# The sums of absolute values of the third feed-forward weight, made by VectorE instead of ScalarE

## What is computed

```python
def _quantize(w):
    gamma = jnp.mean(jnp.abs(w))
    return jnp.clip(jnp.round(w / (gamma + EPS)), -1.0, 1.0)
def _bitlinear(x, w):
    return jnp.matmul(x, _quantize(w).T)
...
x1 = _bitlinear(x, w1)
x2 = _bitlinear(x, w2)
hidden = jax.nn.sigmoid(x1) * x2
return _bitlinear(hidden, w3)
...
x = _layernorm(x + _L0_attn_ref(x, Wq, bq, Wk, bk, Wv, bv, Wo, bo), axis=-1)
x = _layernorm(x + _L0_ffn_ref(x, w1, w2, w3), axis=-1)
```

## Time and profile before

| what | us |
|---|---|
| median of 3 runs | 677.97 |
| lowest and highest run | 674.71, 678.23 |
| the profiled execution | 679.64 |
| its span in the trace | 677.7 |
| TensorE busy in it | 628.8 |
| VectorE busy | 465.6 |
| ScalarE busy | 353.4 |
| GpSimd busy | 133.8 |

### The profile page before, as it was taken

How to read it: one execution, slowest core, us unless ns; L and a number is a source line. 1 busy time by engine, 2 the same in 40 slices (tenths; PEclk the granted TensorE clock), 3 DMA queues, 4 the chain that set the end, 5 groups by cost and what they waited for, 6 DMA issues and landing times.

```text
span 677.7 us, 10688 instructions
## 1 busy us (share of the span) xinstructions
PE 628.8 (93%) x3342; PEld 343.6 (51%) x3342; DVE 465.6 (69%) x795; ACT 353.4 (52%) x814; POOL 133.8 (20%) x148
## 2 busy tenths in 40 slices
PE   6767858799999999999999999999999999999996
PEld 2544545435656565534556565534656565544442
DVE  2767676568877985567878885678878885655333
ACT  2677695514857674313767584313767575303320
POOL 1209678321000400022000400122000400110001
PEclk9689998999999999999999999999999999999999
DMA  7660523020221120021221130020231110000001
GB/s 272 222 222 24 209 60 128 1 59 4 68 93 29 48 78 1 34 70 26 58 88 44 34 92 1 32 71 25 55 86 49 28 36 0 28 21 15 1 1 62
DMA packets 20509, 41.95 MB, mean 62 GB/s; under 512 B 4704, under 2 KB 5856, under 8 KB 19936
## 3 DMA queue, kind: packets, MB, share of 16 engines
q1 hardware_dynamic: 19488, 39.86, 19.3%
q10 hardware_dynamic: 960, 1.33, 0.5%
HBM read 20.20 MB, written 4.19 MB: 36 GB/s over the span
## 4 chain that ended last, share of the span: by engine, by line
PE 76%; DVE 9%; issue 6%; ACT 3%; DMA 3%; SPq 1%; POOL 1%; DVEq 0%; POOLq 0%; ACTq 0%
PE t_ps L1010 15%; PE b_ps L970 11%; PE a_ps L970 11%; PE c_ps L1063 8%; PE a_ps L924 7%; PE s_ps L999 7%; PE a_ps L985 6%; PE b_ps L985 5%; PE a_ps L948 2%; DMA late<-in_w 2%; DVE sh_sb L738 2%; SPq L310 1%; DVE stat L698 1%; ACT p_sb L508 1%; DVE late L728 1%
## 5 line engine op out<-in xcount | busy, mean ns | idle before, releaser
L508 ACT ACTIVATE p_sb<-s_ps,sh_sb 128x512 f32<-128x512 f32 x240 | 164.4, 688 | 86.3 <-DVE sh_sb L738 86.2
L738 DVE TENSOR_REDUCE sh_sb<-s_ps 128x1 f32<-128x512 f32 x240 | 157.5, 679 | 1.9 <-PE s_ps L999 1.9
L1010 PE MATMUL t_ps<-table_sb,p_sb 128*128 128x128 f32 x1024 | 140.4, 281 | 19.4 <-ACT pt_sb L516 16.7
L1010 PEld LDWEIGHTS t_ps<-table_sb,p_sb 128*128 128x128 f32 x1024 | 120.9, 144 | 59.1 <-ACT p_sb L508 24.8
L745 DVE COPY pt_sb<-t_ps 128x512 f32<-128x512 f32 x128 | 88.2, 689 | 85.8 <-PE t_ps L1010 84.3
L516 ACT ACTIVATE pt_sb<-t_ps 128x512 f32<-128x512 f32 x128 | 76.4, 597 | 57.9 <-PE t_ps L1010 56.1
L999 PE MATMUL s_ps<-k_st,q_st 128*128 128x512 f32 x240 | 90.3, 458 | 4.3 <-DVE k_st L659 2.5
L970 PE MATMUL a_ps<-late,q 128*128 128x512 f16 x344 | 81.6, 380 | 2.0 <-DVE late L674 2.0
L970 PE MATMUL b_ps<-late,q 128*128 128x512 f16 x352 | 83.5, 380 | 0.0
L385 POOL TENSOR_TENSOR rot<-raw,table_sb 128x512 f32<-128x512 f32 x20 | 25.5, 1277 | 248.4 <-ACT raw L475 233.3
L924 PE MATMUL a_ps<-xT_sb,wq_sb 128*128 128x512 f32 x128 | 63.1, 624 | 7.6 <-DMA wq_sb<-in_wq 6.3
(11 more groups left out here) (96 smaller groups left out, 623.9 us busy)
## 6 DMA issues: line engine op xcount, KB each, us to landing
q_st<-hi SPq DMA_DIRECT2D x128, 64.0 KB, 2.0
q_st<-lo SPq DMA_DIRECT2D x128, 64.0 KB, 2.0
late<-in_w SPq DMA_DIRECT2D x2, 2816.0 KB, 12.0
xT_sb<-in_xT SPq DMA_DIRECT2D x8, 512.0 KB, 4.7
late<-in_x SPq DMA_DIRECT2D x4, 1024.0 KB, 5.5
out<-late SPq DMA_DIRECT2D x16, 256.0 KB, 2.0
late<-in_w SPq DMA_DIRECT2D x2, 1408.0 KB, 7.2
wo_sb<-in_wo SPq DMA_DIRECT2D x1, 1024.0 KB, 5.7
```

Of the source, the lines that this page charges most:

```text
L508: act.activation(p_sb[:, h % 2, t, :], score_bank(b, n), ACT.Exp, bias=sh_sb[:, n % (2 * SR):n % (2 * SR) + 1], scale=-1.0, accum_out=sums ...
L738: dve.tensor_reduce(sh_sb[:, n % (2 * SR):n % (2 * SR) + 1], score_bank(b, n), AX.X, ALU.min).then_inc(maxed, 1)
L1010: mm = pe.transpose(t_ps[k % 2][:, t * P:(t + 1) * P], p_sb[:, h % 2, t, k * P:(k + 1) * P], id_sb)
```

## The change

The third weight's four sums leave ScalarE's program. VectorE gets a function `abs3_sum`, a TENSOR_REDUCE with absolute value over a piece, and runs it in pairs at the end of its heads 9 and 10. It counts on a semaphore of its own, and TensorE's `total(2)` waits for that one. No elementwise result is written any more for this weight. The sums of the first two weights stay where they were.

```diff
-ABS_AT = [0, 0, 1, 1, 2, 3, 4, 5, 9, 9, 10, 10]
+ABS_AT = [0, 0, 1, 1, 2, 3, 4, 5]
+ABS3_AT = [9, 9, 10, 10]
...
+        abs3_summed = sem("abs3_summed")
...
+            def abs3_sum(c):
+
+                if c == 0:
+                    dve.wait_ge(w_ffn[2], 16)
+                dve.tensor_reduce(asum[:, 2, c:c + 1], piece(stage[2], c, SUMS), AX.X, ALU.add,
+                                  apply_absolute_value=True).then_inc(abs3_summed, 1)
+
...
+                    if h in ABS3_AT:
+                        abs3_sum(ABS3_AT.index(h))
+                        abs3_sum(ABS3_AT.index(h) + 1)
                     if h in TOTAL_AT:
                         thresholds(TOTAL_AT.index(h))
...
-                pe.wait_ge(abs_summed, (n + 1) * SUMS)
+                if n < 2:
+                    pe.wait_ge(abs_summed, (n + 1) * SUMS)
+                else:
+                    pe.wait_ge(abs3_summed, SUMS)
```

## The result

The changed kernel takes 682.17 us (median of 5 runs, 681.75 to 683.72) against 677.62 for the kernel before (5 runs, 674.71 to 678.23). The ratio is 1.0093 with a 95% interval of 1.0074 to 1.0112: slower by a little under 1%, and clear of the scatter. By the medians the change costs 4.1 to 4.6 us, where +3.6 was forecast, and both medians lie inside the range of 677.5 to 686.0. The ratio of the first session would even make 6.3 us (5.0 to 7.6 by its interval), that of the second 4.3 (2.9 to 5.7); with five runs of the kernel before in the first, the size of the loss is known to about a microsecond and not better.

What follows compares the result with a forecast made beforehand. It took TensorE, busy 93% of the span, as the bound, with ScalarE's sums on period 0's chain before 134 us. Terms 3.04 + 0.52 + 0 gave +3.56 us on 677.97: 681.6 us, range 677.5 to 686.0.

Steps and rivals of the forecast that it cites:

- The price of a reduction: On VectorE: each 128x1408 absolute-value reduction estimated at 1.60 us from smaller PSUM reductions, a pair at 3.04 us.
- The order of the work: Head 9: VectorE's pair stands between the halves of q3 and head 10's row maximum, delaying head 10 by 3.04 us.
- For head 10 it said 0.52: Second pair on VectorE delays head 11's row maximum; only 0.52 us more, as VectorE was previously ahead of ScalarE.
- The sum of 3.56: Heads 9 and 10 together: 3.04 + 0.52 + 0 for the clock, +3.56 us in all.
- The clock term: TensorE's wider gap may shift low clock by a head, 0.9 us either way (+2.7 to +4.5); no net change taken.
- its starting point, 677.97: Median of the runs before the change, on which the forecast was put; the profiled execution took 679.64 us.
- The pairs of sums therefore cost 2.21 us in each head, 4.42 in all: Cost of ScalarE's sums on the path, from comparing heads 9 and 10 with heads 13 and 14.
- The prediction's own paragraph on head 9: Head 9: VectorE's row maximum for head 10 ran beside ScalarE's sums; afterwards pair and maximum queue on VectorE, +3.04 us.
- the rival: Relief wins: pairs fall into VectorE idle time, heads 9 and 10 shrink to 8.49 and 4.14; -4.42, 673.5 us; chance 0.07.
- the collision: New VectorE reductions collide with GpSimd's second-weight rounding, each growing 1.1 us; +2.2 to +4.5, 683.8 to 686.1 us; chance 0.10.
- The clock giving most of it back: TensorE's clock full for both heads where it is low now: change only +1.8 us, 679.8 us; chance 0.17.
- The signs named at the end: Changed profile: reductions about 1.6 us, head 9 13.7, head 10 about 6.9, ScalarE waiting some 5, period 1 onward unchanged.

Runs made afterwards that it cites:

- filler2: Changed kernel with seven extra products on TensorE, five in its gap in head 10 and two in head 11: 679.71 us, 1.0043 to the kernel before.
- before_filler: Kernel before with four extra products on TensorE, two in its gap in head 10 and two in head 11: 676.38 us, ratio 1.0003.
- the second profile: Another profiled execution of the unedited changed kernel, timed again beside the experiments: median 681.05 us, 1.0064 to the kernel before; heads 9 to 14 take 45.20 us.
- second session: The changed kernel without an edit timed again, with the experiments: 681.05 us (6 runs) against 676.99 for the kernel before (17 runs), ratio 1.0064.
- short1: Kernel before with ScalarE's first pair of sums, in head 9, over 4 of 1408 columns only: 676.70 us, ratio 0.9999.
- no_sums: Changed kernel with the third weight's sums left out and a constant set by one memset instead: 677.12 us, 1.0001 to the kernel before.
- short2: Kernel before with ScalarE's second pair of sums, in head 10, over 4 of 1408 columns only: 676.52 us, ratio 1.0004.
- act9_gap13: Against the kernel before: first pair on ScalarE in head 9, second in VectorE's wait in head 13, output-bias addition ahead of third weight's rounding: 676.67 us, ratio 1.0008.
- doubled: Changed kernel with each of the four reductions made twice, the first time into a spare tile: 688.41 us, 1.0187 to the kernel before.
- dve9_act10: Changed kernel with the second pair of sums back on ScalarE in head 10, the first on VectorE in head 9: 680.05 us, 1.0060 to the kernel before.
- filler: Changed kernel with fifteen extra products on TensorE, eleven in its gap in head 10 and four in head 11: 683.23 us, 1.0107 to the kernel before.
- gap9: Changed kernel with its first pair of sums moved between the second row maximum and the copy in VectorE's head 9: 681.53 us, 1.0070 to the kernel before.

## Why the prediction was right, point by point

The price of a reduction was worked out at 1.60 us and a pair at 3.04; they took 1603 to 1609 ns and 3.05. The order of the work, and so +3.04 in head 9, came out as 3.04, and 3.02 with the clock held. For head 10 it said 0.52 at full clock; filler2 against before_filler shows 0.56. The sum of 3.56 stands against 3.57 in the profiles (44.33 less 40.76), and 3.54 with clock and collision equal. The second of these is the test; that the first comes out to 0.01 is luck, as two terms of the clock cancel in it.

The clock term was kept at zero between -0.9 and +0.9. The first profile of the changed kernel shows a low clock one head earlier and full for the transposes of head 11, which is +0.9 and -0.9 at once; the second profile shows +0.9 alone (45.20, which is +4.44). The medians, 4.1 to 4.6 us apart, lie nearer to the second. The working looked for the clock in heads 10 and 11 only. It had no term for the stretch from head 15 to period 1, where the first profile loses another 1.13 us at low clock and the second loses none; from head 9 to period 1 the profiles are 4.71 and 4.45 us over that of before, the first just beyond the upper end of +4.5. These low-clock stretches change place between executions of one kernel, and no run shows that the change itself lengthens them. So the 0.5 to 1 us by which the medians exceed the sum may be the clock, but that is not shown: the second session's interval (+2.9 to +5.7 us) takes in the sum, the first session's (+5.0 to +7.6) does not. That the forecast of 681.6 us came so near to 682.17 rests in part on its starting point, 677.97, which is above every later median of the kernel before.

One step of the working failed, without harm to the sum. "The pairs of sums therefore cost 2.21 us in each head, 4.42 in all" compared head 9 with head 13, and overlooked that head 9 also has the halves of q3 on VectorE, 0.45 and 1.81 us, which head 13 lacks. short1 shows the first pair at no cost; the difference of 2.21 was the halves (VectorE is busy for 6.46 us in head 9 and 4.28 in head 13). The prediction's own paragraph on head 9 had the fact, that VectorE's work ran beside ScalarE's sums, and did not carry it back. It did harm to the rival: with the sums moved out of the way altogether, head 9 can't come down to 8.49 us, and no_sums, with no sums at all, takes 677.1 and not 673.5.

Of the rivals, the collision is excluded for the new reductions. A collision of another pair, the copy of the reciprocals with the rounding of the third weight, was there before and after, and was in no sum. With the clock full it costs 1.2 us in head 12 by itself (5.91 in no_sums and 5.92 in short2, 4.68 where the copy starts first). In the profiles of before and changed the clock is low at the start of the head as well (0.86 and 0.87 over the head), the copy is ready later and takes only 0.67 and 0.73 us, and the head is no longer for it. The change moves both partners by the same time, and head 12 takes 5.90 and 5.91, so it cancels. The clock giving most of it back did not happen in either profile.

The signs named at the end held: head 9 at 13.7 us, head 10 at 6.9 (where the clock is full), ScalarE waiting 5.72 us for a row maximum, the stretch from period 1 on unchanged.

What stays open: short2 and act9_gap13 have heads 9 to 14 that are 1.9 and 1.5 us shorter than those in the profile of before, and show it in no median. For short2 the column on the right gives most of the answer: it loses 1.06 us again between head 15 and period 1, at a clock of 0.87, and the 0.85 that is left is within the interval of its median (0.9985 to 1.0024). For act9_gap13 1.46 us are left, which its interval does not cover. The kernel before has one profile, whose 679.64 us are more than 2 us over its medians in the three groups. It took longer ahead of head 9 than any other of the fourteen, 81.30 us, which accounts for most of that; whether its heads 9 to 14, with the clock at 0.50 in head 11, are typical, only a second profile would show.

## What to carry to other kernels

When work moves from one engine to another, ask which engine comes last at that point of the program, not which is busier on the page: here ScalarE's first pair of sums stood beside VectorE work of nearly equal length and was free, and on VectorE the same pair stood behind that work and cost its full length. To price a piece of work by comparing two rounds of a loop, list first everything else that differs between them. And a wait of an engine is only room for work whose data is there: a pair was hidden in head 13, and another gained nothing in the middle of head 9, where its DMA landed too late.

## What the runs showed of the hardware

A fp32 reduction with absolute value of 128x1408 from SBUF takes 1.606 us on VectorE with GpSimd at work or idle (doubled), and a pair 3.05 up to the start of the next instruction; the ABS activation with its accumulator takes 1.38 us per piece on ScalarE, 1.36 from start to start (before). A VectorE copy of 128x512 took 0.43 us when it started 0.04 us ahead of a GpSimd step, and 1.44 when it started 0.20 behind one; on GpSimd's side the loss is 0.25 (dve9_act10 and no_sums). A fp32 product with 512 columns on TensorE is two records and 0.87 us at the full clock (filler). The third weight, 2816 KB, lands 9.4 to 9.5 us after its DMA is issued (changed, gap9).
